# Split q and k laid out in DRAM as six product rows: more packing transfers, plain loads

## The reference

```python
q = elu(q) + 1; k = elu(k) + 1              # 16 heads of 8 features
attn_num   = einsum('bhid,bhjd->bhij', rope(q), rope(k))
attn_denom = einsum('bhid,bhjd->bhij', q, k)
attn_weights = attn_num / attn_denom
out = einsum('bhij,bhjd->bhid', attn_weights, v)
```

## Time and profile before

| | us |
|---|---|
| median of 3 runs | 4204.29 (4202.71 to 4212.35) |
| profiled execution, its own time | 4196.47 |
| its span, first to last instruction | 4194.5 |
| PE busy | 3514.4 (84%) |
| ACT busy | 3228.1 (77%) |
| DVE busy | 2902.8 (69%) |
| POOL busy | 1500.8 (36%) |
| mean granted TensorE clock | 0.916 |
| DMA, mean of 16 engines busy | about 40% |

### The profile page before, as it was taken

How to read it: one execution, slowest core, us unless ns; L and a number is a source line. 1 busy time by engine, 2 the same in 40 slices (tenths; PEclk the granted TensorE clock), 3 DMA queues, 4 the chain that set the end, 5 groups by cost and what they waited for, 6 DMA issues and landing times.

```text
span 4194.5 us, 39166 instructions
## 1 busy us (share of the span) xinstructions
PE 3514.4 (84%) x11446; PEld 1492.4 (36%) x11446; DVE 2902.8 (69%) x3513; ACT 3228.1 (77%) x4037; POOL 1500.8 (36%) x758
## 2 busy tenths in 40 slices
PE   3877598988889898988889898898989888898857
PEld 1131243433333343333334333333334333333423
DVE  2426568768686767868686777858677786858592
ACT  2667588887888787888878888888878888786653
POOL 1112244435243443524344342524434252414361
PEclk9586699999999999999999999999999999998977
DMA  3131244444444444444443444434444444434432
GB/s 120 37 120 58 96 127 147 134 140 129 133 135 126 137 140 130 132 130 136 129 143 122 144 130 131 137 124 141 129 138 133 132 139 133 129 109 135 133 122 86
DMA packets 184390, 526.88 MB, mean 126 GB/s; under 512 B 19217, under 2 KB 66162, under 8 KB 184178
## 3 DMA queue, kind: packets, MB, share of 16 engines
q1 hardware_dynamic: 184178, 524.38, 39.5%
HBM read 488.65 MB, written 38.01 MB: 126 GB/s over the span
## 4 chain that ended last, share of the span: by engine, by line
PE 42%; DVE 16%; ACT 13%; issue 11%; DMA 10%; SPq 7%; POOL 1%; ACTq 0%; POOLq 0%; DVEq 0%
PE bank L782 13%; DMA bc<-bcscr 6%; PE bank L771 4%; PE bank L673 4%; PE bank L734 4%; ACT L1022 4%; ACT rPool L884 3%; SPq L583 3%; DMA kpk<-kscr 3%; PE bank L773 3%; PE bank L712 3%; PE bank L772 3%; DVE ws L1220 3%; SPq L584 3%; PE bank L707 3%
## 5 line engine op out<-in xcount | busy, mean ns | idle before, releaser
L782 PE MATMUL bank<-hF,wst 128*128 128x512 f32 x2304 | 1200.8, 637 | 39.5 <-DVE tmp L1178 34.0
L884 ACT ACTIVATE hF<-bank,cols 128x512 f32<-128x512 f32 x1152 | 770.6, 686 | 362.4 <-PE bank L773 352.7
L1108 DVE TENSOR_TENSOR rPool<-bank,rPool 128x512 f32<-128x512 f32 x1024 | 699.7, 683 | 500.6 <-PE bank L712 470.5
L1313 POOL TENSOR_TENSOR acc<-acc,tmp 128x512 f32<-128x512 f32 x240 | 428.0, 1783 | 1300.3 <-DVE tmp L1178 1297.7
L1328 POOL TENSOR_TENSOR yM<-yM,ws 128x1024 f32<-128x1024 f32 x240 | 699.7, 2915 | 485.1 <-DVE ws L1227 474.4
L884 ACT ACTIVATE rPool<-bank 128x512 f32<-128x512 f32 x1040 | 573.9, 594 | 254.4 <-PE bank L707 202.8
L771 PE MATMUL bank<-xnH,wst 128*128 128x512 f32 x1152 | 648.3, 563 | 90.0 <-ACT hF L884 69.0
L1022 ACT ACT_TABLE_LOAD x531 | 681.3, 1283 | 9.4
L1220 DVE TENSOR_TENSOR_SCAN ws<-dAs,ws 128x1024 f32<-128x1024 f32 x256 | 674.9, 2636 | 5.9 <-ACT dAs L884 3.4
L712 PE MATMUL bank<-qpk,kpk 48*128 48x512 bf16 x1024 | 424.4, 414 | 257.0 <-DVE rPool L1108 255.7
L782 PEld LDWEIGHTS bank<-hF,wst 128*128 128x128 f32 x2304 | 423.3, 199 | 466.1 <-issue 365.3
(11 more groups left out here) (154 smaller groups left out, 3064.2 us busy)
## 6 DMA issues: line engine op xcount, KB each, us to landing
wst<-wscr SPq DMA_DIRECT2D x288, 768.0 KB, 5.9
bc<-bcscr SPq DMA_DIRECT2D x256, 512.0 KB, 4.1
cB<-gscr SPq DMA_DIRECT2D x256, 256.0 KB, 4.8
qscr<-parts SPq DMA_DIRECT2D x32, 384.0 KB, 9.6
kscr<-parts SPq DMA_DIRECT2D x32, 384.0 KB, 3.0
kpk<-kscr SPq DMA_DIRECT2D x128, 96.0 KB
qpk<-qscr SPq DMA_DIRECT2D x128, 96.0 KB
kpk<-kscr SPq DMA_DIRECT2D x128, 64.0 KB
```

The lines of the kernel that those rows point to most:

```text
L782: pe.matmul(ps[FFN][:, :], w2, hF[:, q % HSLOTS, :], start=(c == 0), stop=(c == FC - 1)).then_inc(s_dn, 1)
L884: return nc.scalar.activation(out_, in_, fn, **kw)
L1108: v.tensor_tensor(rP[:, step % 2, c, :], ps[NUM][:, :], rP[:, step % 2, c, :], ALU.mult).then_inc(s_mul, 1)
```

## The change

The scratch in DRAM now has, for each block, each u and each head group, the 48 rows in the order in which they shall lie in SBUF, so that rows which occur two or three times are stored two or three times. A store (`pk`) is six transfers of 128 KB, one for each product row, in place of one of 384 KB. A load is two plain copies of 48 rows of 4 KB for each u, four in all, in place of twelve. The rows of the contraction come in another order (feature outside, product inside), the same on both sides of the matmul. `N_PK` and `LOADS` set the semaphore counts to match. Bytes loaded stay the same, bytes stored double.

```diff
-LOADS = 6
+LOADS = 2
+ROWS_OF = ((0, 0, 0, 1, 1, 2), (0, 1, 2, 0, 1, 0))
...
-        qscr = nc.dram_tensor("qscr", (NB, 2, PARTS, P, 512), BF16, kind="Internal").ap()
-        kscr = nc.dram_tensor("kscr", (NB, 2, PARTS, P, 512), BF16, kind="Internal").ap()
+        qscr = nc.dram_tensor("qscr", (NB, 2, NK, HD * 6, NC * 512), BF16, kind="Internal").ap()
+        kscr = nc.dram_tensor("kscr", (NB, 2, NK, HD * 6, NC * 512), BF16, kind="Internal").ap()
...
+        N_PK = 16 * 6
...
-                    scratch = qscr if n == 0 else kscr
-                    sp.dma_start(scratch[b, u].rearrange("a p t -> p a t"), parts[:, u, :, :]).then_inc(s_pk[u], 16)
+                    scratch = (qscr if n == 0 else kscr)[b, u].rearrange("g (d r) x -> (g d) r x", r=6)
+                    for r in range(6):
+                        sp.dma_start(scratch[:, r, :], parts[:, u, ROWS_OF[n][r], :]).then_inc(s_pk[u], 16)
...
-                heads = slice(HALF * (k % 2) + 32 * (k // 2), HALF * (k % 2) + 32 * (k // 2) + 32)
+                group = 2 * (k % 2) + k // 2
                 for u in range(2):
-                    qs = qscr[b, u, :, heads, :].rearrange("a (d c) t -> a d (c t)", c=NC)
-                    ks = kscr[b, u, :, heads, :].rearrange("a (d c) t -> a d (c t)", c=NC)
-                    for r, part, many in ((0, 0, 3), (3, 1, 2), (5, 2, 1)):
-                        here = slice(HALF * u + HD * r, HALF * u + HD * (r + many))
-                        sp.dma_start(kpk[here, k % 2, :], ks[0:many]).then_inc(s_k_ld[k % 2], 16)
-                        sp.dma_start(qpk[here, k % 2, :], qs[part:part + 1].broadcast_to([many, HD, NC * 512])).then_inc(s_q_ld[k % 2], 16)
+                    rows6 = slice(HALF * u, HALF * u + USED)
+                    sp.dma_start(kpk[rows6, k % 2, :], kscr[b, u, group]).then_inc(s_k_ld[k % 2], 16)
+                    sp.dma_start(qpk[rows6, k % 2, :], qscr[b, u, group]).then_inc(s_q_ld[k % 2], 16)
...
-                        act.wait_ge(s_pk[slot], floor(16 * (2 * b + t // 2)))
+                        act.wait_ge(s_pk[slot], floor(N_PK * (2 * b + t // 2)))
```

More of the change, by code:

```diff
@@ L565, in pre @@
                     settled(sp)
-                    scratch = qscr if n == 0 else kscr
-                    sp.dma_start(scratch[b, u].rearrange("a p t -> p a t"), parts[:, u, :, :]).then_inc(s_pk[u], 16)
+                    scratch = (qscr if n == 0 else kscr)[b, u].rearrange("g (d r) x -> (g d) r x", r=6)
+                    for r in range(6):
+                        sp.dma_start(scratch[:, r, :], parts[:, u, ROWS_OF[n][r], :]).then_inc(s_pk[u], 16)
             def load_heads(b, k):
                 if k == 0:
-                    sp.wait_ge(s_pk[0], floor(32 * (b + 1)))
+                    sp.wait_ge(s_pk[0], floor(N_PK * 2 * (b + 1)))
                     settled(sp)
-                    sp.wait_ge(s_pk[1], floor(32 * (b + 1)))
+                    sp.wait_ge(s_pk[1], floor(N_PK * 2 * (b + 1)))
                     settled(sp)
```

## The result

| | before | after |
|---|---|---|
| median, us | 4203.5 (4196.35 to 4212.35, 4 runs) | 4020.89 (4015.53 to 4022.61, 4 runs) |
| profiled execution, its span | 4194.5 | 4017.3 |
| mean granted TensorE clock | 0.916 | 0.931 |

The ratio is 0.9562, with a 95% interval of 0.9542 to 0.9583: 183 us less by the medians, 177 by the spans of the profiled executions. A second set of runs of both kernels gave 4020.29 and 0.9568 (0.955 to 0.9586). The forecast was 160 us less, 4044; the time lies in its range.

The account below looks back on a forecast made before the run. No engine alone bounds the kernel; the chain changes engines, with waits around loads on few DMA engines. 48 + 89 + 14 + 37 = 188 us, less 28, gives 160 us gained: 4044 us median, range 3995 to 4118.

Parts of the forecast that it names:

- How few engines carry a load: Loads of q and k: three or four DMA engines work; spread over 16, a load takes 6 us, not 16.9.
- The rival in which that copy doesn't spread: 48-row load copies stay narrow, so only the issues get shorter: 4104 us; 9 in 100.
- Place A: PE before the scores of group 2: waits for kpk go, 31 us, plus 17 of slow clock, 48 us.
- Place B: DVE's wait for bc at a block's head: 5.0 us gained 13 times, 65, plus 24 of slow clock, 89 us.
- Place C: DVE in the middle of the block, behind the load for group 0: 14 us gained.
- The starts: First three blocks, waiting for store and load in a row: 14 us, plus 23 of waits behind loads, 37 us.
- The discount: 15%, 28 us, taken off the whole 188 us for what the next wait in line takes back.
- The clock: PE's slow granted clock behind two waits: 17 us at Place A and 24 at Place B gained.
- the sum: All gains over the profiled execution, 48 + 89 + 14 + 37 = 188 us, before 15% is taken off.
- The rival with POOL: At Place B DVE needs POOL's third addition, so its 89 us fall away: 4109 us; 17 in 100.
- The stores: Five more issues a store on SP, last bytes out 3.8 us later; hidden in blocks unless PE waits for weights.
- the rival in which a store's issue grows with its rows: A 128-row store transfer takes 2.0 us to issue, a store 12, delaying weights and gate rows: 4248 us; 4 in 100.

Follow-up runs that it names:

- e3: Kernel before, old scratch and single store kept, each load cut into 24 transfers of 8 rows: 4060.97 us, ratio 0.9666.
- e4: Kernel before with old loads, plus five stores a tile in the new form into a scratch nobody reads: 4211.86 us, ratio 1.0022.
- e2: Changed kernel, each 48-row copy cut into 46 and 2 rows (46/2), eight transfers a load: 4406.1 us, ratio 1.0489.
- e1: Changed kernel, each 48-row copy cut into 33 and 15 rows (33/15), eight transfers a load: 4027.1 us, ratio 0.9584.
- e7: Changed kernel, loads of groups 0 and 1 (loaded ahead) cut 33/15, those of groups 2 and 3 cut 46/2: 4173.09 us, ratio 0.9933.
- e5: Changed kernel, each 48-row copy cut into 34 and 14 rows, eight transfers a load: 4281.62 us, ratio 1.0186.

## Why the prediction was nearly right, and where it was not

- **How few engines carry a load: right.** The DMA share while a load goes through went from 0.24 to 0.83. Issue times were 0.41 us a piece where I took 0.35, and 0.62 a store where I took 0.7. The last kpk piece is there some 6.8 us after a load's first issue (0.9 for the issues between and 5.9 to landing), where I took 6. The rule of the Trainium skill (DMA: Bandwidth & Descriptors, "Why a DMA increments its semaphore by 16 and not by 1") foretold which of 33/15 and 46/2 would be the fast one, and the times agree, 4027 against 4406 us; so does 0.83 for a plain copy of 48 rows. The rival in which that copy doesn't spread is refuted. The Trainium skill's advice to coalesce small transfers (same page, "Rules for kernel authors"), taken alone, would have spoken against e3, which gains 141 us.
- **Place A: right.** 14 waits with 31.3 us are gone.
- **Place B: right.** DVE is idle 0.91 us until POOL's first addition, in all 13 blocks. 70.7 us for DMA and 5.8 for POOL before, 11.9 in all now: 64.6 us gained, 65 forecast.
- **Place C: right.** L1216's idle time fell from 100.6 to 14.1 us. Of these 86.5, 64.6 are B's and 8.2 the third start's (10.44 to 2.23): 13.7 for C.
- **The starts: right in sum, 37.0 us,** though differently divided: the loads' own waits gave 14.9, and a wait of 2.23 us for bc and 0.40 for weights stayed.
- **The discount: the right size by luck.** "I take 15% off, 28 us, for what the next wait in line takes back" had no row behind it, and no wait was named. Yet there is one: PE's wait for DVE's `tmp` behind B went from 34.0 to 62.6 us, 28.6 more. No DMA wait is left in the blocks, so this is not a transfer but DVE, whose work takes longer beside POOL's.
- **The clock: too small; this is the term that was mis-sized.** The waits that went are 31.3 + 64.6 + 13.7 + 37.0 = 146.6 us, against 147 in the sum. Less the new wait that is 118.0, and PE's idle time fell by 121.1 (680.1 to 559.0). The rest of the span's 177.2 us is PE's busy time, which fell by 56.1 for the same matmuls, where the sum had 17 + 24 = 41 for the clock behind A and B. So of the 17 us by which the profiled execution came out below the 4036.5 forecast, 15 are the clock's. The sum priced it behind A and B alone. By PE's busy time, mean of twelve blocks, it gave 1.6 us behind A (1.2 in the sum), 1.8 between there and B (nothing in the sum) and 2.5 behind B (1.9); 1.7 went again behind the new wait.
- **The last 6 us are scatter.** The forecast of the median added 7.8 us to the profiled execution; in the kernel after the two are 1.4 apart. With the 17 that makes the 23 us between 4044 and 4020.9.
- **The rival with POOL: refuted, and mispriced.** 188 less 89 is 99, and less the same 15% 84, so its time would be 4120 us and not 4109, just past the range's end at 4118.
- **The stores: cost about right.** The starts' term had 3 x 3.8 = 11 us for later stores, e4 shows some 9; the rival in which a store's issue grows with its rows is refuted by 0.62 us for 128 rows.

## What to carry to other kernels

Look at how many DMA engines a transfer keeps busy (share and GB/s in a window where it runs alone), before you count transfers or bytes: a slow transfer also delays what is queued behind it, and it is there that most of the 183 us lay. A percentage taken off for "the next wait" is no estimate: follow every engine past the wait that goes, with its own speed when its neighbours run beside it, and name what comes next. Here DVE was the next, 2.2 us in every block. Price a short standing wait of PE with the slow clock behind it, read from windows at either level, and not with its length alone.

## What was unexpected on the chip

- **A very narrow load holds its issuer.** In e2 one issue on SP takes 3.49 us where 0.28 is usual, and 4.17 at most. In each of the 64 loads the last kpk transfer takes over 1 us. In e1, with as many transfers of 33 and 15 rows, none for kpk takes over 0.72. In the kernel before, with 68 rows on the busiest engine, none takes over 0.83, so it isn't every narrow load; what holds SP isn't shown.

The issues of `kpk` in e2 (ns, min/median/max):

```profile
L585 SPq DMA_DIRECT2D kpk<-kscr x256: 223/290/4172, 69.3 to 3931.2; - x128
```

- **A wait of 6.2 us costs 10.4.** In e7 it is 146 us over 14 waits. Behind the wait the granted clock is 0.50, the level of 1.2 GHz, for some 6 us before it is back at 1.00 (2.4 GHz), though PE is busy throughout. The windows behind the wait that ended at 1511.91 (5 x 0.50 + 5 x 0.09 = 3.0 us lost, of 55 / 14 = 3.9 in the mean):

```profile
1512.00:1517.00 5.00, 5.00 (x8) 2.32 (x8) 0.76 (x1) 0.00 (x0) 0.76 (x1) 0.50 0.11 42
1517.00:1522.00 5.00, 5.00 (x17) 3.25 (x16) 1.82 (x3) 3.30 (x5) 0.97 (x1) 0.91 0.15 32
1522.00:1527.00 5.00, 5.00 (x16) 2.48 (x16) 2.19 (x3) 4.92 (x7) 0.30 (x1) 1.00 0.46 178
```

- **Four rows more on the busiest engine cost some 70 us** (e5 against e4), 32 of them slow clock.
- **DVE slows beside POOL.** The scan of L1220 takes 2.28 us in the median with POOL idle and 2.77 with POOL adding, in one trace. So the end of a wait can lengthen the work behind it.
